# K and Q by seven quadrant products, with V's phase storing split sums of x

## The reference, cut to what matters

```python
# x: 8 x 512 x 1024, weights 1024 x 1024, 16 heads of 64, all f32
q, k, v = x @ Wq.T, x @ Wk.T, x @ Wv.T          # per head
q = q * minimum(cond, 4)
scores = where(causal, q @ k.T / 8, lowest)
o = softmax(scores) @ v
y = o @ Wo.T
res = x + absmax_quantised(y) @ ternary(Wffn).T + bias
```

## Time and profile before

| | |
|---|---|
| median of 3 runs | 2060.3 us (2057.4 to 2060.49) |
| the profiled execution, its own time | 2057.48 us |
| its span, first to last instruction | 2055.7 us |
| V's phase, about | 0 to 330 us |
| the steps, about | 317 to 1590 us |
| busy: PE, DVE, ACT, POOL | 97%, 69%, 54%, 42% |
| moved by DMA | 282 MB, mean 137 GB/s |

### The profile page before, as it was taken

The page is one execution under the profiler, slowest core; times in us unless marked ns, Lnnn a source line. Parts: engine busy times, 40 slices in busy tenths (PEclk is TensorE's granted clock), DMA queues, the critical chain, the costliest instruction groups (busy, mean ns, idle before and its releaser), DMA issues.

```text
span 2055.7 us, 34723 instructions
## 1 busy us (share of the span) xinstructions
PE 1988.6 (97%) x10074; PEld 1619.1 (79%) x10074; DVE 1411.2 (69%) x3277; ACT 1115.7 (54%) x2497; POOL 872.2 (42%) x816
## 2 busy tenths in 40 slices
PE   8999999999999999999999999999998999999998
PEld 6888887888877888877888877888886777777775
DVE  6667776777777777778777777777776645545454
ACT  4554445777777777777777777777774000000000
POOL 0344333444435444435445435445443544444442
PEclk9999999999999999999999999999999999999999
DMA  6676645533543533543533543533553432333322
GB/s 204 225 232 219 203 170 183 156 112 114 141 149 103 159 107 105 155 148 103 151 115 102 158 149 103 154 112 102 158 153 101 130 120 94 107 108 100 114 92 82
DMA packets 200981, 282.43 MB, mean 137 GB/s; under 512 B 11216, under 2 KB 146384, under 8 KB 199760
## 3 DMA queue, kind: packets, MB, share of 16 engines
q1 hardware_dynamic: 200384, 281.07, 44.9%
q10 hardware_dynamic: 528, 0.52, 0.1%
HBM read 178.79 MB, written 69.21 MB: 121 GB/s over the span
## 4 chain that ended last, share of the span: by engine, by line
PE 47%; issue 27%; POOL 15%; DVE 5%; DMA 3%; ACT 2%; SPq 1%; POOLq 1%; DVEq 0%; ACTq 0%
POOL prob L273 9%; PE proj_ps L508 8%; PE s_ps L508 8%; PE t_ps L869 7%; PE proj_ps L174 6%; PE o_ps L869 6%; POOL parts L365 5%; PE o_ps L579 5%; DMA k_sw<-k_st 2%; PE o_ps L317 1%; PE t_ps L283 1%; DVE prob L254 1%; DVE parts L365 1%; PE t_ps L557 1%; PE s_ps L808 1%
## 5 line engine op out<-in xcount | busy, mean ns | idle before, releaser
L174 PE MATMUL proj_ps<-parts 128*128 128x512 f32 x3072 | 839.2, 407 | 6.0 <-POOL parts L365 3.6
L273 POOL TENSOR_TENSOR prob<-prob,row_inv 128x128 f32<-128x128 f32 (+3 forms) x512 | 383.1, 748 | 693.5 <-DVE row_inv L267 690.9
L174 PEld LDWEIGHTS proj_ps<-parts 128*128 128x128 f32 x3072 | 538.8, 189 | 112.1 <-POOL parts L365 13.3
L261 ACT ACTIVATE prob<-prob,row_min 128x128 f32<-128x128 f32 (+3 forms) x512 | 287.5, 561 | 145.8 <-DVE row_min L254 139.5
L254 DVE CUSTOM_DVE_ANT_0 prob<-s_ps,mask 128x128 f32<-128x128 f32 (+3 forms) x512 | 248.2, 485 | 56.5 <-PE s_ps L243 22.1
L297 ACT ACTIVATE pt_hi<-t_ps 128x128 fp32r<-128x128 f32 (+3 forms) x512 | 220.7, 431 | 112.2 <-PE t_ps L283 108.2
L564 ACT ACTIVATE yt_q<-t_ps 128x1024 bf16<-128x1024 bf16 x32 | 32.7, 1023 | 427.1 <-PE t_ps L557 427.1
L304 DVE TENSOR_TENSOR pt_lo<-t_ps,pt_hi 128x128 fp32r<-128x128 f32 (+3 forms) x512 | 249.0, 486 | 16.7 <-ACT pt_hi L297 12.5
L283 PE MATMUL t_ps<-ident,prob 128*128 128x128 f32 x1280 | 227.4, 276 | 31.9 <-DVE pt_lo L304 29.4
L365 POOL TENSOR_TENSOR parts<-x_raw,parts 128x512 fp32r<-128x512 f32 x128 | 183.4, 1434 | 18.1 <-ACT parts L359 18.1
L508 PE MATMUL proj_ps<-parts,o_parts 128*128 128x512 f32 x768 | 188.2, 400 | 2.6 <-issue 2.6
(11 more groups left out here) (118 smaller groups left out, 2880.3 us busy)
## 6 DMA issues: line engine op xcount, KB each, us to landing
x_raw<-xT SPq DMA_DIRECT2D x128, 512.0 KB, 5.7
v_scratch<-v_out SPq DMA_DIRECT2D x64, 512.0 KB, 3.3
k_sw<-k_st SPq DMA_DIRECT2D x128, 256.0 KB, 4.7
v_st<-v_scratch SPq DMA_DIRECT2D x128, 256.0 KB, 4.2
oT_scratch<-o_sum SPq DMA_DIRECT2D x64, 256.0 KB, 2.5
x_raw<-oT_scratch SPq DMA_DIRECT2D x32, 512.0 KB, 4.8
x_tile<-x SPq DMA_DIRECT2D x32, 512.0 KB, 5.4
out<-res SPq DMA_DIRECT2D x32, 512.0 KB, 3.2
```

The lines of the kernel that those rows point to most:

```text
L174: mm = pe.matmul(out, l, r, start=(k == 0 and i == 0), stop=(k == KT - 1 and i == 2))
L261: act.activation(prob[:, u % 4, 0:w], prob[:, u % 4, 0:w], ACT.Exp, bias=row_min[:, u % 4:u % 4 + 1], scale=-1.0, accum_out=row_sum[:, u % ...
L273: pool.tensor_tensor(prob[:, u % 4, 0:w], prob[:, u % 4, 0:w], row_inv[:, u % 4:u % 4 + 1].broadcast_to([P, w]), ALU.mult).then_inc(norm_d ...
```

## The change

- K and Q are projected by the same seven-product scheme as V. x of a batch is cut in two halves of the inner dimension and into tokens, a weight group in two by two quadrants. A product is 4 slices by 3 passes, 12 matmuls of 256 columns; K and Q take 14 products, 168 matmuls a step (`project`, L209). Two PSUM banks hold them in turn; `qk_copy` on ACT (8 a step) and `qk_add` on DVE (6 a step), each 128 by 256, combine them into `k_sum` and `q_sum` in SBUF. `evac_hi` and `evac_lo` read these instead of PSUM.
- The steps no longer split x. V's phase stores each of its seven split operands (`store_xv`, 0.5 MiB each, 16 pairs by 7) to `x_scr`. For the two plain pairs the operands are made later, beside pairs 9 to 12 (`AGAIN`, `parts_after`). A step loads its batch's seven operands, 1 MiB each in rows of 8 KB (`load_xq`, L403), each into the place of the operand that Q's product of the step before has just used.
- V is stored as it is, 16 MiB for 32; `split_v` on POOL splits it in the steps, two instructions of 128 by 256 for each head.
- The weights' quadrant sums are made on POOL (`w_first_sums`, `w_last_sums`), 7 splits of 128 by 512 for each of K and Q (`split_w`) stand for 4 of 128 by 1024.
- Scores start later: on PE a step n holds units 14 and 15 of step n-2, then 0 to 13 of step n-1. All 16 units of the last step come after the last projection.
- `o_lower` writes to `o_sum`, the loads of x in V's phase are rows of 1 KB for 512 B, and memory is laid out anew.

```diff
-            passes = [(w_lo[w][:, k, col], x_hi[:, k, :]), (w_hi[w][:, k, col], x_lo[:, k, :]),
-                      (w_hi[w][:, k, col], x_hi[:, k, :])]
-            for i, (l, r) in enumerate(passes):
-                mm = pe.matmul(out, l, r, start=(k == 0 and i == 0), stop=(k == KT - 1 and i == 2))
...
+        ORDER = [A11, A12, S2, S1, S3, S4, A22]
+        M_P1, M_P2, M_P6, M_P5, M_P7, M_P3, M_P4 = range(7)
+        ON_OTHER = (M_P2, M_P5, M_P3)
...
+            for k in range(half * CH // 2, (half + 1) * CH // 2):
+                passes = [(1, 0), (0, 1), (0, 0)]
+                for i, (wp, xp) in enumerate(passes):
+                    mm = pe.matmul(qk_bank(w, m), wc[w][:, c, wp, k, :], xq[:, c, :, xp, k, :],
+                                   start=(fresh and k == 0 and i == 0), stop=(k == CH - 1 and i == 2),
+                                   skip_group_check=(not fresh))
...
+        def load_xq(sp, it, b, m):
+            c = ORDER[m]
+            if isinstance(it, int) and it == 0:
+                sp.wait_ge(v_product_done, V_LAST + (3, 3, 4, 4, 5, 5, 6)[c])
+            else:
+                sp.wait_ge(product_done, (it - 1) * 14 + 7 + m + 1)
+            sp.dma_start(xq[:, c, :, :, :, :].rearrange("p j a k s -> p (j a k s)").bitcast(F32),
+                         x_scr[bass.ds(b, 1), c, :, :, :, :].rearrange("b p j a f -> p (b j a f)"))\
+              .then_inc(x_in[c], 16)
...
+            pool.tensor_tensor(hi, v_raw[:, :, h, :], one[:, 0:1].rearrange("p (a b) -> p a b", b=1)
+                               .broadcast_to([P, QT, DH]), ALU.mult).then_inc(v_hi_done, 1)
+            pool.wait_ge(v_hi_done, it * HG + h + 1)
+            pool.tensor_tensor(lo, v_raw[:, :, h, :], hi.bitcast(F32), ALU.subtract).then_inc(v_lo_done, 1)
...
+        AGAIN = {9: 0, 11: 1}
...
+        def store_xv(sp, e, c):
+            sp.wait_ge(xv_lo_done, SPLIT_COUNT[e, c])
+            sp.dma_start(x_scr[e[0] // 2, c, :, e[0] % 2, :, :], xv[:, c, :, :].bitcast(F32)).then_inc(xv_stored[c], 16)
...
+            if STORE_COUNT[e, c] > 1:
+                eng.wait_ge(xv_stored[c], (STORE_COUNT[e, c] - 1) * 16)
```

More of the change, by code:

```diff
@@ L1105, in v_dve @@
             wv_sums(dve)
-            for q in range(4):
-                v_low(dve, 0, q)
             ws_low(dve, S4)
@@ new lines, in act_step @@
+            W(0)
+            E(14)
+            WO(1)
+            H(12)
+            E(15)
+            W(1)
+            WO(2)
+            H(13)
+            OL(2)
+            E(0)
+            copy(now, K, COPY_U)
+            H(14)
+            E(1)
+            copy(now, K, COPY_P5)
+            W(2)
+            WO(3)
+            if old and not older:
+                for slot in v_stored:
+                    act.wait_ge(slot, PAIRS * 16)
+            H(15)
+            evacuate(old, K, 1)
@@ L1335, in act_step @@
+            E(2)
+            H(0)
+            evacuate(old, Q, 1)
+            E(3)
+            W(3)
+            H(1)
+            OL(3)
+            E(4)
+            W(4)
+            WO(4)
+            H(2)
+            copy(now, K, COPY_C21)
+            E(5)
+            W(5)
+            WO(5)
             H(3)
+            copy(now, Q, COPY_P1)
             E(6)
-            if now and old:
-                x_high(act, n, 6)
-            if late_for is not None:
-                split_w_qk(act, o, late_for, 3, False)
@@ L1354, in act_step @@
             H(7)
+            if now and not old:
+                for slot in v_stored:
+                    act.wait_ge(slot, PAIRS * 16)
+            evacuate(now, K, 0)
             E(10)
@@ L1431, in W, with OA, add, evacuate @@
+            def OA(h):
+                if h >= 2 and older:
+                    o_add(dve, older[0], h)
+                elif h < 2 and old:
+                    o_add(dve, old[0], h)
+            def add(w, which):
+                if now:
+                    qk_add(dve, now[0], w, which)
+            def evacuate(step, w, blk):
+                if step:
+                    evac_lo(dve, step[0], w, blk)
+            def W(m):
                 if qk_for is not None:
[L1432 removed]
+                    split_w(dve, 2 * qk_for, m, True)
+                if late_for is not None:
+                    split_w(dve, 2 * late_for + 1, m, True)
@@ L1448, in dve_step @@
+            I(3)
+            M(4)
+            W(3)
+            L(1)
+            add(K, ADD_C12)
+            OA(3)
+            I(4)
+            M(5)
+            W(4)
+            WO(4)
+            L(2)
+            evacuate(old, Q, 1)
+            if now and old:
+                batch_scale(dve, now[0], now[2])
+            I(5)
+            M(6)
+            W(5)
+            WO(5)
             L(3)
```

1255 lines of the change are left out of this document (646 added, 609 removed).

## The result

| | before | after |
|---|---|---|
| time, median | 2059.7 us | 2126.7 us (2120.6 to 2132.6) |
| ratio to before | | 1.0325, 95% interval 1.0294 to 1.0356 |
| span of the profiled execution | 2055.7 us | 2120.6 us |
| mean granted clock | 0.996 | 0.970 |

The account below looks back on a forecast made before the run. PE was taken to set the pace in V's phase and the steps. Terms of -70, 0, +9, +5, +5 and +20 sum to -31 on 2057.5 us, 2026.5, or 2028 us for the median; range 1972 to 2088.

Parts of the forecast that it names:

- projections: Steps on PE: 168 matmuls at 0.117 us replace 96 at 0.228, 2.2 us a step, -70 us over 32 steps.
- splitting and combining, waits in a steady step: Steady steps: ACT -2.0 us, DVE +0.5, POOL unchanged, none on the path; 2.3 us of waits on `pt_low` stay: 0 us.
- K's exchanged copy: Step ends: copy lands 4.4 to 5.5 us after issue, read at 5.7, just in time; 0.3 us a step, +9 us.
- steps with weights: Seven such steps, with more splits on DVE and sums on POOL, cost 21 us against 16 now: +5 us.
- end of the steps: After the last projection: all 16 units, for 10, and eight splits of Wo, for six, are exposed there: +5 us.
- V's phase: Pairs 2 to 14: DMA must move 95 MB in 248 us; at 345 GB/s it runs late, mostly in pairs 9 to 12: +20 us.
- rival A: Steps: K's copy lands 8.0 us after issue, 2.3 us late in every step, costing 71 us; 2089 us, chance 0.12.
- Rival E: Projections on PE: matmuls of 256 columns take 0.130 us in rows of 12, so a step gains nothing; 2097 us, chance 0.03.
- rival D: Steps: PE's waits on `pt_low` fall from 2.3 to 0.3 us, another -62 us; 1965 us, chance 0.18.
- B: Steps: DVE becomes the bound through contention with POOL, steps back at 38 us, the 70 us gone; 2097 us, chance 0.07.
- Rival C: V's phase: bound by DMA outright at 305 GB/s, +55 us for +20; 2062 us, chance 0.13.

Follow-up runs that it names:

- e1: Kernel after the change, with SP issuing K's copy of block 0 ahead of the step's fifth load of x instead of behind it: 2068.5 us.
- e12: e1 with the next x's splits in pairs 10 and 12 held back, and in pairs 9 and 11 its load issued earlier and first split later: 2052.9 us.
- e5: e1 with every second tile of x stored in V's phase with 64 of 512 columns only, the steps reading the first tile twice: 2065.7 us, one execution.
- e2: Kernel after the change, with K's copy of block 0 issued by ACT ahead of unit 12's exponential instead of by SP behind five loads of x: 2221.1 us.

## Why the prediction was wrong

| term | predicted | found | by |
|---|---|---|---|
| projections | -70 | about -55 | starts 0.120 us apart; steady step 36.0 for 38.0 in e1 |
| splitting and combining, waits in a steady step | 0 | -9 | 0.3 us a step: PE idle 0.6 us in e1, 0.9 before; DVE 27.1 us a step, 29.0 expected |
| K's exchanged copy | +9 | +51 | kernel after against e1, 31 steps |
| steps with weights | +5 | +12 | e1: 9.0 us over steady in each of 3 groups (27), before 15 |
| way into the steps | not in the sum | +22 | 29.5 less the shift of 8; waits of 18.2 us, the rest mostly clock |
| end of the steps | +5 | +13 | last column, 6.3, and the 6.8 us of projections that left it |
| V's phase | +20 | +26 | first column |

The found sizes add up to +60 us, the spans differ by 64.9. The 5 us between lie in the 31 steps; I have not separated them.

**The step that failed is "just in time, and I take 0.3 us a step for when it is not".** The times around it were right: the copy is issued where I had it, and PE wants it 5.6 us later (5.7 in the prediction). I put the landing at 4.4 to 5.5 us, reckoning that a load takes 2.5 us, so that 1 to 1.5 us of the fifth would be left. The five loads took 7.0 to 9.6 us each to land, overlapping, and the fifth landed 5.8 us behind the copy's issue. The copy's second half took 6.6 to 8.1 us in the steps above, 5.0 to 8.2 over the 30 that have such loads ahead of it. PE waited in 23 steps, 45.9 us in all, and I had 9. The row that answered, 8.0 us behind loads of x, was in the prediction as rival A, with a chance of 0.12; I gave it away to an estimate made from the local peak of 414 GB/s, which is not even one of 8 KB rows alone: 329 of its 549 packets are shorter. Around the copy the kernel after moved some 310. A was right in its mechanism. Its price (2.3 us in every step, 71 in all) was too high for the waits and left out the clock: in a long step the copy cost 5 us (41.0 for 36.0), of which 2.9 to 3.3 were the wait.

**Projections.** The forecast was right in kind. e1 shows a steady step of 36.0 us, inside the 35.5 to 36.5 that I gave. The size is that of my lower end: 168 x 0.120 = 20.2 us against 21.9, 1.7 a step, 55 in all; the other 0.3 us a step is in waits. Rival E (0.130) and rival D (the waits go) were wrong, and so was B: the splits of K and Q that now read two operands from SBUF took 0.69 and 0.82 us, where they took 0.69 and 0.75 with one in PSUM before (I had added 0.19 to each), and DVE has a quarter of the step free. The contention of DVE and POOL that the Trainium skill names (GPSIMD Engine Reference, Specifications) did not lengthen them to a size that matters here.

**The way into the steps** was missing from the sum. In step 0 there are no units between the products, so PE asks for seven loads of x, weights, and K's copy within 15 us. PE waited 5.3, 0.5 and 0.9 us for x in it, and then 11.5 us for K's first copy, which took 15.0 us to land (the longest in the run). A change that adds 1 MB loads to every product should have been costed where products are closest together, not only in the steady step.

**The end of the steps** cost 13 us and not 5: PE's waits there are 23.0 us (for DVE's `pt_all`, `row_min` and the splits of Wo, and for POOL), for 9.6 before. The last column alone, 6.3, would look like a hit.

**V's phase** came near in size, +26 for +20, and in place ("pairs 9 to 12"), and was wrong in cause, so the size was mostly luck. I had divided bytes by a bandwidth. From pair 4 to 8 the DMA share is about 1.0 and a pair takes 19.0 to 19.3 us; two stalls of some 10 us come from ACT standing on a load that can't be issued before its buffer comes free. e12 (same bytes, 16 us less) shows it, and e5 (no backlog, same stall) fits. Rival C, the outright bound, is out, and so are the 345 GB/s that I took: pairs 11 and 12 of e12 moved 400 and 403.

Order: e1's one moved line and e12's order of loads and splits bring the change from 2126.7 to 2052.9 us. What it brings by its seven products is then still mostly paid back: some 19 us on the way into the steps (41.9 from V's end to the first scores, for 15.2, less the shift of 8), 10 in V's phase, 12 in the steps with weights, 13 at their end.

## What to carry over

A small transfer that PE reads soon after it is issued must be costed by what is in flight when it is issued, and compared with the slack that it has: here the copy took no longer than before, and its slack fell from 12.3 to 5.6 us. It helped to let the queue that issues the bulk wait for the small one's data and send it first (e1); another engine's queue without that wait made it worse (e2). An engine that splits ahead for later work must not have a load's first reader in front of what the current product needs: count from when the buffer comes free, plus the landing time, to where the reader stands. Cost the first pass through a loop by itself, since there the same transfers come without the work that spaces them.

## What the runs showed of the chip that I had not expected

- A wait of 3.3 us before the scores was followed by about 4 us at a granted clock of 0.50; one of 1.7 us left it at 1.00. In the long steps a late transfer was thus paid one and a half times (5 us for 3.3). The length of the wait alone doesn't decide it. In the kernel after, the clock stayed at 1.00 behind waits of 2.77 and 2.40 us, and behind one of 1.69 us it was 0.62 in the next 4.5 us. What decides stays open, and so does why the copy lands in 6.6 or 8.1 us with the same order of issues. Windows behind the first and the last of these waits:

```profile
429.30:433.80 4.50, 4.47 (x35) 4.36 (x36) 1.93 (x7) 1.86 (x7) 2.61 (x4) 1.00 0.83 342
1284.20:1288.70 4.50, 4.28 (x19) 3.98 (x20) 4.30 (x12) 2.41 (x7) 2.00 (x3) 0.62 0.93 382
```

- The same half copy landed in 3.8 us where SP had issued nothing for 5.4 us (e1), 6.6 to 8.1 behind five loads on its own queue, and 9.6 (median) from another queue with six loads moving (e2). The Trainium skill (DMA: Bandwidth & Descriptors, Queues, rings and completion order) has each DMA engine take turns between the queues, a packet at a time. Equal shares of some 400 GB/s would have brought the copy's two halves of 256 KB through sooner than that (an estimate: 0.52 MB at 200 GB/s is 2.6 us, for 1.3 alone, so some 5 us to landing); no run tells whether the length of the rows is why it was not so.
- Pairs of V's phase kept their 19.04 us at a DMA share of 1.0. The share says that the DMA engines are occupied, not that anything is late.
